# A layernorm head with its residual adds in line, and a softmax normaliser whose Ln and Exp stand two steps apart

## The chip, the cores and the metric

The kernel runs on all 8 cores of one Trainium2 chip. Each core computes one of the 8 batch elements and they exchange nothing. The time is the device time of the slowest core in microseconds (us).

## What is computed

Per batch element x is 2048 tokens by 1024 features. The layer is an attention block on the normalised x, then a three-matrix linear block with tanh on the normalised result, each added back:

```python
x = x + attn(layernorm(x))
#   attn(x): q, k, v = x@Wq, x@Wk, x@Wv in 16 heads of 64
#            softmax(q k^T / 8) v, heads joined, then x + out @ Wp
x = x + ffn(layernorm(x))
#   ffn(x): tanh(((x @ W1) @ W2) @ W3 + bias)
```

The attention block adds its own input back, so after it x holds x + layernorm(x) + out @ Wp.

## The kernel before

Everything lies transposed on the chip, features on the partitions. `xr` is the f32 residual in 8 blocks of 128 features by 2048 tokens; `S`, `qb`, `kb` and `vt` hold bf16 of the same size. The program is written by hand with one counting semaphore for each engine: TE (TensorE, PE in the profile), VE (VectorE, DVE), SE (ScalarE, ACT), GP (GpSimd, POOL) and SP. Each engine works its own queue in program order, so an instruction that waits holds back all that stand behind it on its engine.

**Head.** `layernorm` sums x and its square over the features with matmuls against ones, and gets mean and rstd for all 2048 tokens (rstd by Ln and Exp on ACT, L253 and L255). Then it goes over 8 blocks j: subtract the mean (L264, DVE), multiply by rstd (L280, or L272 for j of 5 and over, DVE), cast into `S` (L282 or L274, ACT), add the normalised block to the residual (L284, DVE), and 8 matmuls of the first quarter of Wq (L290, PE). For j = 5, 6, 7 the product goes to three spare f32 buffers in `kb`, and the add to the residual is left for after the loop (L310). The first copies of the projected q (L306, L307, ACT) wait for the last of these matmuls, and for `s_ve.n`, the last DVE instruction issued up to that point. The subtraction of j = 0 is queued ahead of DVE's wait for rstd. The other quarters of Wq, then Wk, Wv and a bound for the exponent follow. The first write to `kb` by the K projection waits for the adds that were left.

**Attention loop.** 512 iterations in the order (c, p, m): 4 chunks c of 512 query tokens, 8 head pairs p, 16 blocks m of 128 keys. Iteration t issues on ACT exp(t), the 128x1024 exponential (L866); on PE the scores of t+2 (L628, L632, called qk here), then the products with V (L878, L883, called pv) and the sums of the exponentials (L888, L891, called dn) of t. Scores and exponentials have two slots each, by the parity of m. So exp(t+2) needs qk(t+2) and dn(t), and qk(t+2) needs exp(t).

After m = 15 of a head pair DVE copies the two accumulators out (L899, L901). I call this a boundary; there are 32, the last of them behind the loop. pv of the next m = 0 waits for both copies. In the iteration m = 1 that follows, `_norm` is called: ACT gets Ln (L906) and Exp (L908) of the sums, which makes their reciprocal, and DVE multiplies (L914) and writes the bf16 result `ao`.

**Side work.** When the last pair of a chunk is normalised, the rest of the layer for that chunk is put in two lists that are worked off in the next chunk: 8 output projections (`wp_q`, L650) and 55 pieces in `work_q`, of which an even share is emitted by iteration number (`budget`). The first piece flushes all of `wp_q`, so the 8 projections come as one burst of 64 matmuls, at m = 2 of p = 0. By the formula for `budget`, of the later pieces these stand near a boundary, by p and m: statistics at m = 0 and 2 of p = 1 and 2; `emit_apply` (two blocks, each L754 and L757, DVE) at p = 3, m = 0, 3 and 5, all of which the first W1 projection at m = 7 needs (L776, PE); projections at m = 1 and 3 of p = 4 and 5 (L776) and at m = 1 of p = 6 (L794); a Tanh piece (L807, ACT) at p = 6, m = 4 and at p = 7, m = 2. For the last chunk the same work runs after the loop.

Lines as numbered in the kernel before:

Of the kernel before, what the change touches and what calls it, by code (L numbers as in the profile page):

```python
# [17 lines left out]
NCH = D // 128  # L18
# [33 lines left out]
def build_program(upto=99, dbg=False):  # L52
# [19 lines left out]
    with ctx:  # L72
# [143 lines left out]
        def layernorm(src_f32_j, dst_bf16, add_back, dma_gate=False, wq0=False):  # L216
# [7 lines left out]
            with nc.psum_tensor(_nm("ln_mean"), [128, 2048], F32) as mps, \  # L224
                 nc.psum_tensor(_nm("ln_sq"), [128, 2048], F32) as sps:
                mm_mark = [0, 0]
                for j in range(NCH):
# [9 lines left out]
                    for n4 in range(4):  # L237
# [17 lines left out]
                rstd_mark = s_se.inc(SE.activation(rstd_sb, rstd_sb, AF.Exp,  # L255
                                                   bias=0.0, scale=-0.5))
            def _normalize(wq0_pj):
                wsl0 = use_wquarter(0) if wq0_pj is not None else None
                mkq0 = 0
                deferred = []  # L260
                for j in range(NCH):
# [4 lines left out]
                    if j == 0:  # L266
                        VE.wait_ge(s_se.h, rstd_mark)
                    if add_back:
                        sl2 = j % 2
                        if j >= 5:  # L270
                            buf = kbf[:, 2048 * (j - 4):2048 * (j - 3)]
                            m = s_ve.inc(VE.tensor_mul(buf, tmpf, rstd_sb))  # L272
                            SE.wait_ge(s_ve.h, m)
                            cast_mark[sl2] = s_se.inc(SE.copy(dst_jj, buf))  # L274
                            VE.wait_ge(s_ve.h, m)
                            deferred.append((src_jj, buf))
                        else:
                            if cast_mark[sl2]:
                                VE.wait_ge(s_se.h, cast_mark[sl2])
                            m = s_ve.inc(VE.tensor_mul(tmpf2pp[sl2], tmpf, rstd_sb))  # L280
                            SE.wait_ge(s_ve.h, m)
                            cast_mark[sl2] = s_se.inc(SE.copy(dst_jj, tmpf2pp[sl2]))  # L282
                            VE.wait_ge(s_ve.h, m)
                            m = s_ve.inc(VE.tensor_add(src_jj, src_jj, tmpf2pp[sl2]))  # L284
                            VE.wait_ge(s_ve.h, m)
                        if wq0_pj is not None:
                            TE.wait_ge(s_se.h, cast_mark[sl2])
                            for half in range(2):
                                for n4 in range(4):
                                    ins = TE.matmul(  # L290
                                        wq0_pj[half][:, 512 * n4:512 * (n4 + 1)],
                                        wsl0[:, j, 128 * half:128 * (half + 1)],
                                        dst_bf16[:, 2048 * j + 512 * n4:
                                                 2048 * j + 512 * (n4 + 1)],
                                        start=(j == 0), stop=(j == NCH - 1),
                                        skip_group_check=True)
                            mkq0 = s_te.inc(ins)
                    else:
                        m = s_ve.inc(VE.tensor_mul(dst_jj, tmpf, rstd_sb))
                        VE.wait_ge(s_ve.h, m)  # L300
# [7 lines left out]
                add_done = 0  # L308
                for src_jj, buf in deferred:
                    add_done = s_ve.inc(VE.tensor_add(src_jj, src_jj, buf))  # L310
                    VE.wait_ge(s_ve.h, add_done)
                return (ev0, ev1, add_done)
# [44 lines left out]
        wproj(0, S_ap, qb_ap, q0=1, ev_init=ln_evs[:2])  # L357
# [4 lines left out]
        with nc.psum_tensor("pk0", [128, 1024], F32) as pk0, \  # L362
# [49 lines left out]
            for q in range(4):  # L412
                widx = 4 + q
                wsl = use_wquarter(widx)
                for jj in range(2):
                    j = 2 * q + jj
                    for hf in range(2):
# [14 lines left out]
                        if j == 0 and hf == 0 and ln_evs[2]:  # L432
                            SE.wait_ge(s_ve.h, ln_evs[2])
# [147 lines left out]
        with nc.psum_tensor("sc0", [128, 1024], F32) as sc0, \  # L581
# [274 lines left out]
            pending_norm = []  # L856
            TE.wait_ge(s_ve.h, s_ve.n)
# [3 lines left out]
            for t, (c, p, m) in enumerate(iters):  # L861
# [33 lines left out]
                if m == NM - 1:  # L895
# [8 lines left out]
                    def _norm(cp=c, pp=p, dncp=dn_cp):  # L904
                        SE.wait_ge(s_ve.h, dncp)
                        m1 = s_se.inc(SE.activation(dr, dr, AF.Ln, bias=0.0, scale=1.0))  # L906
                        SE.wait_ge(s_se.h, m1)
                        m1 = s_se.inc(SE.activation(dr, dr, AF.Exp, bias=0.0, scale=-1.0))  # L908
                        VE.wait_ge(s_se.h, m1)
                        while wp_q:  # L910
                            wp_q.pop(0)()
                        if cp > 0:
                            VE.wait_ge(s_te.h, st["wp_mm"])
                        mm = s_ve.inc(VE.tensor_mul(ao[:, 512 * pp:512 * (pp + 1)],  # L914
                                                    ao_un, dr))
                        if pp == NCH - 1:
                            ao_ready[cp] = mm
                            wp_q.extend(lambda j=j2: emit_wp_j(cp, j) for j2 in range(NCH))
                            work_q_done[0] = 0
                            work_q.extend(tail_thunks(cp, flush=(cp == NCC - 1)))  # L920
                            work_q_len[0] = len(work_q)
                        return mm

                    pending_norm.append(_norm)
                if pending_norm and m == 1:
                    ao_mult_mark = pending_norm.pop(0)()
# [7 lines left out]
            preload_flush_vt()  # L934
            while pending_norm:
                ao_mult_mark = pending_norm.pop(0)()
# [69 lines left out]
```

## Time and profile before

| | us |
|---|---|
| median of the runs shown (2) | 1306.75 (1306.47 to 1307.04) |
| profiled execution | 1306.87 |
| its span, slowest core (core 2) | 1305.2 |
| spans of the 8 cores | 1289.8 to 1305.2 |
| stages of core 2: head up to the first L344 | 0 to 117.8 |
| attention loop | 344 to 1201 |

The span runs from the first to the last instruction of a core; 1.7 us of the profiled execution lie outside it. TensorE is busy 76% of the span, ACT 55%, DVE 32%. In the attention loop chunk 0 (344 to 512 us) has no side work; chunks 1 to 3 take about 230 us each. The granted clock is a share of 2.4 GHz: 1.0 is 2.4 GHz and 0.5 is 1.2 GHz.

### The profile page before, as it was taken

How to read it: one execution, taken by the hardware profiler on the slowest of the kernel's cores; microseconds unless marked ns; L12 is line 12 of the kernel's file. 1: busy time of each engine (PE TensorE's matmuls, PEld its weight loads, DVE VectorE, ACT ScalarE, POOL GpSimd, SP SyncE). 2: the span in 40 equal slices, each digit the busy share in tenths (PEclk: the TensorE clock that was granted, in tenths of full speed). 3: DMA queues.
4: the chain of work that ended last, by engine and by line, in shares of the span. 5: the costliest groups of instructions: out<-in, count | busy, mean ns of one | idle time of the engine just before them, and what ended most of it. 6: DMA issues, size and time to landing. Idle time of an engine off the chain costs nothing.

```text
span 1305.2 us, 15441 instructions; the slowest of 8 cores (1289.8 to 1305.2 us)
## 1 busy us (share of the span) xinstructions
PE 988.1 (76%) x5111; PEld 334.2 (26%) x5185; DVE 415.6 (32%) x558; ACT 724.3 (55%) x702; POOL 66.9 (5%) x80
## 2 busy tenths in 40 slices
PE   3356977987678777787987777798778779976776
PEld 1112423443122222222222222232222223321222
DVE  3695033144510101234222223422222342222454
ACT  0223234101688987497677648766772986687102
POOL 2000000000000000000100010010001001211000
PEclk9768999999698999999999899999888999988878
DMA  9900000022000000401443350055334004593902
GB/s 251 168 1 0 1 1 1 1 33 33 1 1 1 1 1 2 64 1 17 65 58 59 63 65 2 6 63 70 58 65 65 1 2 64 67 161 52 143 1 64
DMA packets 98937, 57.65 MB, mean 44 GB/s; under 512 B 3624, under 2 KB 97840, under 8 KB 97840
## 3 DMA queue, kind: packets, MB, share of 16 engines
q0 software_dynamic: 79040, 39.85, 24.4%
q1 hardware_dynamic: 19824, 16.83, 4.4%
q8 instruction: 46, 0.75, 0.2%
q14 instruction: 27, 0.22, 0.1%
HBM read 88.12 MB, written 8.39 MB: 74 GB/s over the span
## 4 chain that ended last, share of the span: by engine, by line
PE 47%; ACT 17%; DVE 9%; issue 7%; DMA 2%; ACTq 0%; DVEq 0%; POOLq 0%
ACT S L866 14%; PE sc L628 9%; PE pvs L878 9%; PE dns L888 6%; PE lnps L776 4%; PE wps L776 4%; PE pvb L470 2%; PE pva L470 2%; PE wps L650 2%; PE lnps L794 2%; PE lnps L650 2%; DMA wbuf<-wp 2%; PE wps L794 1%; DVE tiny L544 1%; DVE S L899 1%
## 5 line engine op out<-in xcount | busy, mean ns | idle before, releaser
L866 ACT ACTIVATE S<-sc,cbias 128x1024 bf16<-128x1024 f32 x512 | 550.2, 1109 | 188.1 <-PE dns L891 175.4
L628 PE MATMUL sc<-qb,kb 64*128 64x512 bf16 x512 | 200.8, 393 | 121.4 <-ACT S L866 110.5
L878 PE MATMUL pvs<-S,vt 128*64 128x512 bf16 x512 | 212.8, 416 | 26.4 <-DVE S L901 26.4
L883 PE MATMUL pvs<-S,vt 128*64 128x512 bf16 x512 | 213.5, 417 | 0.0
L632 PE MATMUL sc<-qb,kb 64*128 64x512 bf16 x512 | 204.9, 401 | 0.0
L891 PE MATMUL dns<-S,ones 128*64 128x512 bf16 x512 | 202.5, 396 | 0.0
L888 PE MATMUL dns<-S,ones 128*64 128x512 bf16 x512 | 202.4, 395 | 0.0
L628 PEld LDWEIGHTS sc<-qb,kb 64*128 64x128 bf16 x512 | 47.6, 93 | 342.8 <-issue 342.8
L878 PEld LDWEIGHTS pvs<-S,vt 128*64 128x64 bf16 x512 | 54.9, 107 | 149.7 <-issue 149.6
L899 DVE COPY S<-pvs 128x512 f32<-128x512 f32 x32 | 22.1, 692 | 190.4 <-PE dns L891 186.4
L423 PE MATMUL pk<-S,vt 128*128 128x512 bf16 x250 | 57.7, 385 | 2.7 <-PEq L355 2.4
L524 ACT ACTIVATE S<-kb 128x2048 bf16<-128x2048 bf16 x8 | 15.1, 1906 | 76.6 <-PE tp L494 73.9
L139 POOL DMA_DIRECT2D wbuf<-w x36 | 31.5, 876 | 505.5 <-PE sc L632 437.8
L891 PEld LDWEIGHTS dns<-S,ones 128*64 128x64 bf16 x512 | 57.2, 112 | 0.0
L888 PEld LDWEIGHTS dns<-S,ones 128*64 128x64 bf16 x512 | 57.1, 112 | 0.1
L883 PEld LDWEIGHTS pvs<-S,vt 128*64 128x64 bf16 x512 | 55.0, 107 | 0.0
L632 PEld LDWEIGHTS sc<-qb,kb 64*128 64x128 bf16 x512 | 47.5, 93 | 0.0
L344 PE MATMUL pj<-S,vt 128*128 128x512 bf16 x188 | 43.0, 389 | 4.1 <-ACT qb L307 3.9
L434 ACT CAST kb<-pk 128x1024 bf16<-128x1024 f32 x16 | 16.2, 1012 | 51.4 <-PE pk L423 51.4
L807 ACT ACTIVATE S<-S,bias_pp_sb 128x512 bf16<-128x512 bf16 x32 | 23.1, 722 | 38.7 <-DVE S L802 38.6
L650 PE MATMUL wps<-S,wbuf 128*128 128x512 bf16 x97 | 30.7, 464 | 18.2 <-DMA wbuf<-wp 12.0
L290 PE MATMUL pq0a<-S,vt 128*128 128x512 bf16 x31 | 13.3, 568 | 40.3 <-ACT S L282 32.1
(162 smaller groups left out, 1147.1 us busy)
## 6 DMA issues: line engine op xcount, KB each, us to landing
wbuf<-w POOLq DMA_DIRECT2D x36, 512.0 KB, 5.6
xr<-x SPq DMA_DIRECT2D x4, 2048.0 KB, 24.4
out<-xr SPq DMA_DIRECT2D x128, 64.0 KB, 1.7
wbuf<-wp POOLq DMA_DIRECT2D x14, 512.0 KB, 6.0
vt<-w POOLq DMA_DIRECT2D x8, 512.0 KB, 20.4
vt<-wq POOLq DMA_DIRECT2D x4, 512.0 KB, 34.0
vt<-wk POOLq DMA_DIRECT2D x4, 512.0 KB, 47.5
wbuf<-wv POOLq DMA_DIRECT2D x4, 512.0 KB, 30.3
```

The source lines that it names most:

```text
L344: ins = TE.matmul(pj[sl][:, 512 * n4:512 * (n4 + 1)], wsl[:, i, 128 * jj:128 * (jj + 1)], src_bf[:, 2048 * i + 512 * n4: 2048 * i + 512 * ...
L423: ins = TE.matmul(pj[sl][:, 512 * n2:512 * (n2 + 1)], wsl[:, i, 128 * jj:128 * (jj + 1)], S_ap[:, 2048 * i + 1024 * hf + 512 * n2: 2048 * ...
L470: ins = TE.matmul(pvh[h][:, 512 * n2:512 * (n2 + 1)], wsl[:, i, 128 * jj:128 * (jj + 1)], S_ap[:, 2048 * i + 1024 * h + 512 * n2: 2048 * i ...
L628: TE.matmul(scs[sl][:, 0:512], kb[0:64, 2048 * p + 128 * m: 2048 * p + 128 * (m + 1)], qb[0:64, 2048 * p + 512 * c: 2048 * p + 512 * (c + 1)],
L632: ins = TE.matmul(scs[sl][:, 512:1024], kb[64:128, 2048 * p + 128 * m: 2048 * p + 128 * (m + 1)], qb[64:128, 2048 * p + 512 * c: 2048 * p ...
L650: ins = TE.matmul(acc[:], wsl[:, i, 128 * jj:128 * (jj + 1)], ao[:, 512 * i:512 * (i + 1)], start=(i == 0), stop=(i == NCH - 1))
L776: ins = TE.matmul(acc[:], wsl[:, i, 128 * jj:128 * (jj + 1)], rhs_of(i), start=(i == 0), stop=(i == NCH - 1))
L866: ins = SE.activation(p_un[sl], scs[sl][:], AF.Exp, bias=cbias[:], scale=0.125)
L878: TE.matmul(pvs[0:64, :], vt[:, 1024 * m + 128 * p: 1024 * m + 128 * p + 64], p_un[sl][:, 0:512], start=(m == 0), stop=(m == NM - 1), tile ...
L883: TE.matmul(pvs[64:128, :], vt[:, 1024 * m + 128 * p + 64: 1024 * m + 128 * (p + 1)], p_un[sl][:, 512:1024], start=(m == 0), stop=(m == NM ...
L888: TE.matmul(dns[0:64, :], ones64[:], p_un[sl][:, 0:512], start=(m == 0), stop=(m == NM - 1), tile_position=(0, 0), skip_group_check=True)
L891: ins = TE.matmul(dns[64:128, :], ones64[:], p_un[sl][:, 512:1024], start=(m == 0), stop=(m == NM - 1), tile_position=(0, 64), skip_group_ ...
```

## The change

In the head, DVE waits for rstd before the first subtraction and not after it. All 8 blocks take the path that j = 0 to 4 took: product in one of two alternating buffers, cast on ACT, add to the residual at once. The adds after the loop go, and so does the wait of the K projection for them. `SE.wait_ge(s_ve.h, s_ve.n)` ahead of L306 stays; the last DVE instruction issued there is now the add of j = 7, where it was the product of j = 7.

In the attention loop `_norm` is cut in two. Ln is still issued at m = 1. Exp, the wait of DVE for it, the product and, after the last pair of a chunk, the filling of `wp_q` and `work_q` are issued at m = 3, ahead of that iteration's side work. So the burst of output projections comes at m = 3 of p = 0. Behind the loop Ln and the rest run one after the other, as before. The number of instructions of each kind is the same.

```diff
@@ -252,37 +252,26 @@ layernorm
-                rstd_mark = s_se.inc(SE.activation(rstd_sb, rstd_sb, AF.Exp,
-                                                   bias=0.0, scale=-0.5))
+                m = s_se.inc(SE.activation(rstd_sb, rstd_sb, AF.Exp, bias=0.0, scale=-0.5))
+                VE.wait_ge(s_se.h, m)
             def _normalize(wq0_pj):
...
-                deferred = []
                 for j in range(NCH):
...
                     m = s_ve.inc(VE.tensor_sub(tmpf, src_jj, mean_sb))
                     VE.wait_ge(s_ve.h, m)
-                    if j == 0:
-                        VE.wait_ge(s_se.h, rstd_mark)
                     if add_back:
                         sl2 = j % 2
-                        if j >= 5:
-                            buf = kbf[:, 2048 * (j - 4):2048 * (j - 3)]
-                            m = s_ve.inc(VE.tensor_mul(buf, tmpf, rstd_sb))
-                            SE.wait_ge(s_ve.h, m)
-                            cast_mark[sl2] = s_se.inc(SE.copy(dst_jj, buf))
-                            VE.wait_ge(s_ve.h, m)
-                            deferred.append((src_jj, buf))
-                        else:
...
+                        if cast_mark[sl2]:
+                            VE.wait_ge(s_se.h, cast_mark[sl2])
+                        m = s_ve.inc(VE.tensor_mul(tmpf2pp[sl2], tmpf, rstd_sb))
+                        SE.wait_ge(s_ve.h, m)
+                        cast_mark[sl2] = s_se.inc(SE.copy(dst_jj, tmpf2pp[sl2]))
+                        VE.wait_ge(s_ve.h, m)
+                        m = s_ve.inc(VE.tensor_add(src_jj, src_jj, tmpf2pp[sl2]))
+                        VE.wait_ge(s_ve.h, m)
@@ -305,11 +294,7 @@
                 ev0 = s_se.inc(SE.copy(qb_ap[:, 0:2048], wq0_pj[0][:]))
                 ev1 = s_se.inc(SE.copy(qb_ap[:, 2048:4096], wq0_pj[1][:]))
-                add_done = 0
-                for src_jj, buf in deferred:
-                    add_done = s_ve.inc(VE.tensor_add(src_jj, src_jj, buf))
-                    VE.wait_ge(s_ve.h, add_done)
-                return (ev0, ev1, add_done)
+                return (ev0, ev1)
@@ -429,8 +414,6 @@ the K projection
-                        if j == 0 and hf == 0 and ln_evs[2]:
-                            SE.wait_ge(s_ve.h, ln_evs[2])
@@ -901,29 +885,37 @@ the attention loop
-                    def _norm(cp=c, pp=p, dncp=dn_cp):
+                    def _norm_ln(cp=c, pp=p, dncp=dn_cp):
                         SE.wait_ge(s_ve.h, dncp)
-                        m1 = s_se.inc(SE.activation(dr, dr, AF.Ln, bias=0.0, scale=1.0))
-                        SE.wait_ge(s_se.h, m1)
-                        m1 = s_se.inc(SE.activation(dr, dr, AF.Exp, bias=0.0, scale=-1.0))
-                        VE.wait_ge(s_se.h, m1)
-                        while wp_q:
-                            wp_q.pop(0)()
...
+                        lnm = s_se.inc(SE.activation(dr, dr, AF.Ln, bias=0.0, scale=1.0))
+
+                        def _norm_fin(cp=cp, pp=pp, lnm=lnm):
+                            SE.wait_ge(s_se.h, lnm)
+                            m1 = s_se.inc(SE.activation(dr, dr, AF.Exp,
+                                                        bias=0.0, scale=-1.0))
+                            VE.wait_ge(s_se.h, m1)
+                            while wp_q:
+                                wp_q.pop(0)()
+                            if cp > 0:
+                                VE.wait_ge(s_te.h, st["wp_mm"])
+                            mm = s_ve.inc(VE.tensor_mul(ao[:, 512 * pp:512 * (pp + 1)],
+                                                        ao_un, dr))
...
+                            return mm
+                        return _norm_fin
+                    pending_norm.append(_norm_ln)
+                if pending_fin and m == 3:
+                    ao_mult_mark = pending_fin.pop(0)()
                 if pending_norm and m == 1:
-                    ao_mult_mark = pending_norm.pop(0)()
+                    pending_fin.append(pending_norm.pop(0)())
@@ -932,8 +924,10 @@ after the loop
             preload_flush_vt()
+            while pending_fin:
+                ao_mult_mark = pending_fin.pop(0)()
             while pending_norm:
-                ao_mult_mark = pending_norm.pop(0)()
+                ao_mult_mark = pending_norm.pop(0)()()
```

## Rows read from the trace of the kernel before

**Rows 1.** the profile page's first line, of the whole program
```profile
span 1305.2 us, 15441 instructions; the slowest of 8 cores (1289.8 to 1305.2 us)
```

**Rows 2.** the page's chain that ended last, share by engine
```profile
PE 47%; ACT 17%; DVE 9%; issue 7%; DMA 2%; ACTq 0%; DVEq 0%; POOLq 0%
```

**Rows 3.** groups by line: busy us, mean ns, idle before and releaser
```profile
L866 ACT ACTIVATE S<-sc,cbias 128x1024 bf16<-128x1024 f32 x512 | 550.2, 1109 | 188.1 <-PE dns L891 175.4 <-PE sc L632 8.0 <-PE lnps L679 0.3
...
L906 ACT ACT_TABLE_LOAD x9 | 11.5, 1283 | 2.8 <-DVE S L901 2.7
```

**Rows 4.** timeline, VectorE, head: start us, duration, line, tiles, idle before
```profile
60.41 2.29 DVE L280 TENSOR_TENSOR qb<-qb 128x2048 f32<-128x2048 f32 x1 [3.29 <-ACT qb L255]
...
82.12 2.29 DVE L280 TENSOR_TENSOR kb<-qb 128x2048 f32<-128x2048 f32 x1 [0.17 <-DVE qb L264]
...
89.38 2.29 DVE L280 TENSOR_TENSOR qb<-qb 128x2048 f32<-128x2048 f32 x1 [0.17 <-DVE qb L264]
...
96.57 2.29 DVE L272 TENSOR_TENSOR kb<-qb 128x2048 f32<-128x2048 f32 x1
...
106.15 2.29 DVE L272 TENSOR_TENSOR kb<-qb 128x2048 f32<-128x2048 f32 x1
108.55 7.09 DVE L310 TENSOR_TENSOR xr<-xr,kb 128x2048 f32<-128x2048 f32 x3
```

**Rows 5.** the same timeline, ScalarE, end of the head
```profile
108.53 1.90 ACT L274 CAST S<-kb 128x2048 bf16<-128x2048 f32 x1 [2.89 <-DVE kb L272]
114.02 1.87 ACT L306 CAST qb<-pq0a 128x2048 bf16<-128x2048 f32 x1 [3.59 <-PE pq0b L290]
```

**Rows 6.** timeline, all engines, the boundary at 429.8 us
```profile
429.78 0.69 DVE L899 COPY S<-pvs 128x512 f32<-128x512 f32 x1 [16.96 <-PE dns L891]
...
431.36 0.63 ACT L906 ACTIVATE S<-S 128x512 f32<-128x512 f32 x1 [0.54 <-DVE S L901]
...
431.66 0.38 PE L891 MATMUL dns<-S,ones 128*64 128x512 bf16 x1
...
432.09 0.63 ACT L908 ACTIVATE S<-S 128x512 f32<-128x512 f32 x1
...
432.62 2.10 ACT L866 ACTIVATE S<-sc,cbias 128x1024 bf16<-128x1024 f32 x2
...
433.86 0.37 PE L628 MATMUL sc<-qb,kb 64*128 64x512 bf16 x1 [0.95 <-ACT S L866]
...
434.91 2.12 ACT L866 ACTIVATE S<-sc,cbias 128x1024 bf16<-128x1024 f32 x2 [0.19 <-PE dns L891]
```

**Rows 7.** timeline, VectorE: first copy of three other boundaries of chunk 0
```profile
409.10 0.69 DVE L899 COPY S<-pvs 128x512 f32<-128x512 f32 x1 [18.27 <-PE dns L891]
...
449.83 0.69 DVE L899 COPY S<-pvs 128x512 f32<-128x512 f32 x1 [16.32 <-PE dns L891]
...
469.87 0.69 DVE L899 COPY S<-pvs 128x512 f32<-128x512 f32 x1 [16.31 <-PE dns L891]
```

**Rows 8.** busy by stretch: length, PE, PEld, DVE, ACT, POOL, granted clock, DMA
```profile
411.20:414.60 3.40, 3.14 (x14) 0.60 (x12) 0.69 (x1) 2.84 (x4) 0.00 (x0) 0.50 0.00 0
```

**Rows 9.** timeline, all engines, after the boundary at 595.7 us
```profile
600.11 0.69 DVE L914 TENSOR_TENSOR S<-S 128x512 bf16<-128x512 f32 x1
...
600.71 0.68 DVE L754 TENSOR_TENSOR vtmp<-xr,vtmp 128x512 f32<-128x512 f32 x1
...
607.33 1.67 PE L776 MATMUL wps<-S,wbuf 128*128 128x512 bf16 x7 [0.97 <-DVE S L757]
```

**Rows 10.** timeline, TensorE, after the boundary at 622.2 us
```profile
625.30 1.90 PE L776 MATMUL wps<-S,wbuf 128*128 128x512 bf16 x8
...
627.13 0.39 PE L628 MATMUL sc<-qb,kb 64*128 64x512 bf16 x1
```

**Rows 11.** timeline, ScalarE, after the boundary at 708.4 us
```profile
713.67 1.28 ACT L807 ACT_TABLE_LOAD   x1
...
715.59 2.10 ACT L866 ACTIVATE S<-sc,cbias 128x1024 bf16<-128x1024 f32 x2
```

More of the change, by code:

```diff
@@ L265, in _normalize @@
                     VE.wait_ge(s_ve.h, m)
-                    if j == 0:
-                        VE.wait_ge(s_se.h, rstd_mark)
                     if add_back:
                         sl2 = j % 2
-                        if j >= 5:
-                            buf = kbf[:, 2048 * (j - 4):2048 * (j - 3)]
-                            m = s_ve.inc(VE.tensor_mul(buf, tmpf, rstd_sb))
-                            SE.wait_ge(s_ve.h, m)
-                            cast_mark[sl2] = s_se.inc(SE.copy(dst_jj, buf))
-                            VE.wait_ge(s_ve.h, m)
-                            deferred.append((src_jj, buf))
-                        else:
[L278 to L285, printed above, removed]
+                        if cast_mark[sl2]:
[6 more added lines that the diff above has]
+                        VE.wait_ge(s_ve.h, m)
                         if wq0_pj is not None:
@@ L355, in wproj @@
             nc.all_engine_barrier()
-        wproj(0, S_ap, qb_ap, q0=1, ev_init=ln_evs[:2])
+        wproj(0, S_ap, qb_ap, q0=1, ev_init=ln_evs)
         rmax = tiny[:, 0:2]
@@ L856, in build_program @@
             pending_norm = []
+            pending_fin = []
             TE.wait_ge(s_ve.h, s_ve.n)
@@ L902, in build_program @@
                     recip_mark = dn_cp
-                    def _norm(cp=c, pp=p, dncp=dn_cp):
+                    def _norm_ln(cp=c, pp=p, dncp=dn_cp):
                         SE.wait_ge(s_ve.h, dncp)
-                        m1 = s_se.inc(SE.activation(dr, dr, AF.Ln, bias=0.0, scale=1.0))
-                        SE.wait_ge(s_se.h, m1)
-                        m1 = s_se.inc(SE.activation(dr, dr, AF.Exp, bias=0.0, scale=-1.0))
-                        VE.wait_ge(s_se.h, m1)
-                        while wp_q:
-                            wp_q.pop(0)()
[L912 to L922, printed above, removed]
@@ L924, in build_program @@
-                    pending_norm.append(_norm)
+                        lnm = s_se.inc(SE.activation(dr, dr, AF.Ln, bias=0.0, scale=1.0))
[10 more added lines that the diff above has]
+                                                        ao_un, dr))
+                            if pp == NCH - 1:
+                                ao_ready[cp] = mm
+                                wp_q.extend(lambda j=j2: emit_wp_j(cp, j)
+                                            for j2 in range(NCH))
+                                work_q_done[0] = 0
+                                work_q.extend(tail_thunks(cp, flush=(cp == NCC - 1)))
+                                work_q_len[0] = len(work_q)
+                            return mm
```

## The prediction, made before the changed kernel was run

> **What bounds the kernel now.** I read the page's first line, then the chain that ended last, then the groups by line, then the two places that the change touches in the timeline. The slowest core spans 1305.2 us [rows 1]. The chain lies for 47% on PE, 17% on ACT and 9% on DVE [rows 2]: no engine bounds the whole, the work is handed from one to another. So each edit has to be read where it stands.
>
> In the head DVE sets the pace. From block to block it takes 89.38 - 82.12 = 7.26 us, the subtraction, the product and the add of 2.29 us each with their issue. In the blocks that leave the add for later it takes (106.15 - 96.57)/2 = 4.79 us [rows 4]. ACT sits idle 2.89 us before the last cast [rows 5], so the cast waits for DVE.
>
> In chunk 0 of the loop it is a circle of ACT and PE. ACT has exponentials of 1.11 us, idle 188.1 us in front of them in total, 175.4 of it on L891, the dn matmuls [rows 3]. At the boundary at 429.78 [rows 6] the copies run, Ln starts at 431.36, Exp at 432.09, exp(2) at 432.62, qk(4) at 433.86 and exp(4) at 434.91. A boundary period is 469.87 - 449.83 = 20.04 us [rows 7].
>
> **The head, part by part.** *Subtraction behind the wait.* The product of j = 0 starts at 60.41, as soon as Exp is done, its subtraction having run before [rows 4]. Now the subtraction starts there and the product one DVE step later: 7.26 - 4.79 = 2.47 for a step with its wait, 2.4 without; I take 2.4. *Adds in line.* Between the product of j = 5 and that of j = 7 there are now two adds more, 2 x (7.26 - 4.79) = 4.94. The add of j = 4 was in line already and that of j = 7 comes behind the last cast. Together the last cast moves by 2.4 + 4.9 = 7.3, with the waits of the alternating buffers 7.4 us. *The copy L306.* It starts at 114.02, 5.5 us after the last cast [rows 5], and it would also wait for the add of j = 7. That add starts when the cast does and takes 2.3, so it is done first. *The adds taken away at the end.* Those 7.09 us at 108.55 [rows 4] run beside the matmuls and copies of Wq; nothing on the path waited, so nothing comes back. If the path from the cast to Wq had slack, the 7.4 would be less, but PE has only the head's own matmuls to do there and waits for the casts. Head: +7.4 us, between +7.3 and +7.5.
>
> **The loop, a boundary that is bound by latency.** The total of ACT's work stays; what changes is whether it fills a gap. Before, exp(2) waits for Ln and Exp. Without Exp it needs dn(0), which ends at 431.66 + 0.38 = 432.04, and starts 0.1 later, at 432.14 where it was 432.62: 0.48 earlier [rows 6]. Two exponentials in 2.10 us of 1.1 each start 1.00 apart, so exp(3) starts at 433.14 and Exp at 434.14. Exp holds ACT for 432.62 - 432.09 = 0.53, so exp(4) may start at 434.67. By PE it could start at 432.14 + (434.91 - 432.62) = 434.43. ACT decides: 434.67 for 434.91, a gain of 0.24 us, which the circle then carries on. The floor of this gain is 0, if Exp at m = 3 costs what m = 1 saves; the ceiling is Exp's whole 0.53.
>
> **All 31 boundaries inside the loop.** I went through each by the same rows and sorted them.
> - 11 are of this kind (chunk 0 from the fourth on, and those with statistics beside them): 11 x 0.24 = 2.6.
> - 3 in chunk 0 have the clock at 0.50 just behind them [rows 8]: PE decides there and has the earlier start; I take 0.3 each, 0.9.
> - 3 more, two at chunk ends and one with a table load, again set by the chain from exp(2): 0.3 each, 0.9.
> - 3 have a Tanh piece at m = 2. There ACT runs exp(2), a table load, Tanh and exp(3) back to back [rows 11], so exp(3), and behind it PE, come the whole 0.53 sooner: 1.6.
> - 8 have a projection at m = 1 or a long load: qk(4) at 627.13 stands right behind L776, which began at 625.30 [rows 10]. PE is the bound and ACT's 0.53 is worth 0.
> - 3, at p = 3, lose. DVE is the bound there: the product L914 at 600.11 goes between the apply pieces of m = 0 and m = 3, the next of which begins at 600.71, and the projection at 607.33 has PE idle 0.97 for the last L757 [rows 9]. Now L914 waits for Exp at m = 3. By the steps of the clean boundary exp(2) starts 432.14 - 429.78 = 2.36 behind the first copy [rows 6], here at 598.07, exp(3) at 599.07 and Exp at 600.07; Exp takes 0.63 and DVE follows 0.1 behind, at 600.80 in place of 600.11: 0.69 later, and the whole apply chain with it. -0.69 each, -2.1. Bounds: 0 if Exp came no later, -1.2 if exp(3) were late by half a step.
>
> The burst of projections at a chunk's start is issued one iteration later. Its first matmul needs L914, which would end about 0.3 us after PE is free; but PE has then done one iteration more ahead of the burst, so this is within the gain taken. The loads of wp stay where they were.
>
> What is late next: DVE's product comes some 2 us later at every boundary. Behind it on DVE stand only side pieces from m = 3 on; those of m = 1 and 2 now go ahead of it. Its readers are the burst, once a chunk, and the next copies 12 iterations later.
>
> **Sum.** Loop: 2.6 + 0.9 + 0.9 + 1.6 + 0 - 2.1 = 3.9 us gained. Net 7.4 - 3.9 = +3.5. Against the profiled execution of 1306.87, which is 0.12 over the median of the runs, that is **1310.4 us**.
>
> **A rule on tables.** The switch between Ln and Tanh shows 9 loads at L906, 1.283 us each [rows 3]. The load at 713.67 is followed by Tanh and exp(3) 1.92 later, 1.28 and 0.64, with no further hold [rows 11]; and among the 512 exponentials of L866 [rows 3] the view has no load, though they run after Ln and after Tanh alike. So Exp on either side of a Tanh finds its table, and the number of loads stays. The Trainium skill ("ScalarE: Activation LUTs", section "What ACT_TABLE_LOAD costs") gives 2.66 us for every switch, 1.28 of load and 1.38 of drain. The load agrees with the trace, the drain does not show. Were it there, and a switch in each of the 3 places where a Tanh now comes between Ln and Exp, two switches in each would by that page be an estimated 16 us, and the time 1326.
>
> **Rivals.**
> 1. *The loop gives back the full Exp everywhere.* 31 x 0.53 = 16.4, no loss at p = 3: 1306.9 + 7.4 - 16.4 = 1297.9. For it: ACT idles at many boundaries. Against: Exp still takes ACT 0.53 at m = 3, and 8 boundaries are PE's. About 0.07.
> 2. *The split gains nothing, DVE's losses stay.* 1306.9 + 7.4 + 2.1 = 1316.4. For it: the total of ACT's work is the same. Against: exp(2) is plainly held by 0.48. About 0.15.
> 3. *The head's delay is hidden.* 1306.9 - 3.9 = 1303.0. Only if something else held Wq; ACT's idle time before the last cast speaks against it. About 0.05.
> 4. *The tables.* If Exp behind a Tanh wants the table of Ln back, that is two loads in each of 3 places, 6 x 1.28 = 7.7: 1318.1. About 0.03.
> 5. *The clock.* This is the one that ends on the slower side. Place: the iterations just after a boundary. One stretch at 0.50 [rows 8] makes the period 429.78 - 409.10 = 20.68 [rows 6, 7] in place of 20.04, 0.64 more. If ACT's second hold at m = 3 made PE pause twice and brought a new such stretch to all 28 boundaries that I did not count with one, 28 x 0.64 = 18 us: 1328, and 1337 with half as much again where PE is the bound. From 0.81 us lost at each boundary ((26.1 - 3.5)/28) it passes 2%. Against: PE's pauses get shorter, not longer. About 0.06, 0.02 of it past 2%.
>
> The forecast has 0.64. A difference of 2%, about what a measurement of this kernel can tell from no change, is 26 us. Rival 1 is 0.7% faster and rival 2 is 0.7% slower, so nearly all is within it: faster 0.01, same 0.97, slower 0.02. The range for 8 in 10: the forecast with its bounds is 1306 to 1314; reaching to rivals 2 and 3 it is 1303 to 1317.
>
> **What would show it.** L280 for j = 0 at 62.8 and the last cast at 115.9, L306 at 121.4, all seven product starts in between 7.26 apart. At a clean boundary exp(2) about 2.36 after the first copy, where it was 2.84, and exp(4) 4.9 after it, where it was 5.13; a clean period of 19.8. At p = 3, L776 waits 1.7 and more for L757 in place of 0.97. L906 still has 9 loads and L908 none. I would be wrong if L306 moved by less than 7, if the clean period stayed at 20.04 or fell to 19.5, or if the share of half clock in the loop changed, as that is set by PE's pauses and one such stretch is worth as much as two or three boundaries.

## The result

The changed kernel takes 1312.43 us in the median of 17 runs, the kernel before 1307.08 us in 16. The ratio is 1.0037, with a 95% interval of 1.0025 to 1.0049: 4.8 us slower. The medians are of all executions; in some of them the cores of one die were granted a lower clock and the time was up to 9% longer, and the ratios and the means below leave these out. The forecast was 1310.4 us, ratio 1.003, within a range of 1303 to 1317. The sign and the size were right; of the terms behind the sum, the head and five kinds of boundary came out about as worked, and three kinds did not, one of them (p = 0) by no more than its periods scatter.

The page of the changed kernel, its first line and the chain that ended last by engine:

```profile
span 1313.2 us, 15517 instructions; the slowest of 8 cores (1298.7 to 1313.2 us)
...
PE 49%; ACT 15%; DVE 9%; issue 6%; DMA 2%; DVEq 0%; ACTq 0%; POOLq 0%
```

The profiled execution took 1314.77 us and its slowest core is core 7, where before it was core 2 with 1305.2 [rows 1]. The spans of the eight cores of one execution lie some 15 us apart, and which core is the slowest changes from one execution to the next, so I compare the same core or the mean of all eight below. That mean is 1297.4 us in the profiled execution of before and 1305.8 in that of the changed kernel. PE's share of the chain rose from 47% to 49% and ACT's fell from 17% to 15% [rows 2].

Two groups of the groups by line, core 2 of the changed kernel (busy us, mean ns, idle before and releaser):

```profile
L850 ACT ACTIVATE S<-sc,cbias 128x1024 bf16<-128x1024 f32 x512 | 548.8, 1110 | 192.5 <-PE dns L875 178.4 <-PE sc L615 8.4
...
L890 ACT ACT_TABLE_LOAD x9 | 11.5, 1283 | 2.8 <-DVE S L885 2.7
```

ACT's exponentials are as before and the table loads at Ln are still 9 of 1.283 us [rows 3]; there is no load at L894, the Exp that was moved. Where a Tanh now comes between Ln and Exp, ScalarE of the same core shows:

```profile
715.30 1.28 ACT L790 ACT_TABLE_LOAD   x1
716.60 0.72 ACT L790 ACTIVATE S<-S,bias_pp_sb 128x512 bf16<-128x512 bf16 x1
717.23 1.10 ACT L850 ACTIVATE S<-sc,cbias 128x1024 bf16<-128x1024 f32 x1
718.22 0.62 ACT L894 ACTIVATE S<-S 128x512 f32<-128x512 f32 x1
```

The Tanh starts 1.30 us behind the start of its load, and the moved Exp at 718.22 needs none.

**Head.** The timeline of core 2 in the head, VectorE and then ScalarE:

```profile
61.27 2.29 DVE L263 TENSOR_TENSOR qb<-xr,qb 128x2048 f32<-128x2048 f32 x1 [5.48 <-ACT qb L255]
63.67 2.29 DVE L269 TENSOR_TENSOR qb<-qb 128x2048 f32<-128x2048 f32 x1
```

```profile
59.26 1.91 ACT L255 ACTIVATE qb<-qb 128x2048 f32<-128x2048 f32 x1
...
116.79 1.90 ACT L271 CAST S<-kb 128x2048 bf16<-128x2048 f32 x1 [5.36 <-DVE kb L269]
122.50 1.86 ACT L295 CAST qb<-pq0a 128x2048 bf16<-128x2048 f32 x1 [3.81 <-PE pq0b L279]
```

The first subtraction starts at 61.27, when rstd is there; before, the product started at that point [rows 4]. From rstd to the last cast it is 116.79 - 61.27 = 55.52 us, before 108.53 - 60.41 = 48.12 [rows 4, 5]: +7.40. The mean of the eight cores is +7.40 too. The copy of q follows 5.7 us behind the cast, before 5.5 [rows 5].

**A clean boundary**, core 2, the same place in a chunk as [rows 6]:

```profile
452.69 0.69 DVE L883 COPY S<-pvs 128x512 f32<-128x512 f32 x1 [14.01 <-PE dns L875]
...
454.27 0.63 ACT L890 ACTIVATE S<-S 128x512 f32<-128x512 f32 x1 [0.54 <-DVE S L885]
...
455.04 2.12 ACT L850 ACTIVATE S<-sc,cbias 128x1024 bf16<-128x1024 f32 x2
...
456.30 0.37 PE L611 MATMUL sc<-qb,kb 64*128 64x512 bf16 x1 [0.48 <-ACT S L850]
...
457.05 0.63 ACT L894 ACTIVATE S<-S 128x512 f32<-128x512 f32 x1
...
457.57 1.11 ACT L850 ACTIVATE S<-sc,cbias 128x1024 bf16<-128x1024 f32 x1
...
457.78 0.69 DVE L901 TENSOR_TENSOR S<-S 128x512 bf16<-128x512 f32 x1 [3.60 <-ACT S L894]
```

exp(2) starts 455.04 - 452.69 = 2.35 us behind the first copy, before 432.62 - 429.78 = 2.84 [rows 6]. Exp, L894, now stands between exp(3) and exp(4), and exp(4) starts 4.88 behind the copy, before 5.13. The period, from two copies two boundaries apart:

```profile
432.90 0.69 DVE L883 COPY S<-pvs 128x512 f32<-128x512 f32 x1 [14.01 <-PE dns L875]
...
472.48 0.69 DVE L883 COPY S<-pvs 128x512 f32<-128x512 f32 x1 [14.01 <-PE dns L875]
```

(472.48 - 432.90)/2 = 19.79, before 20.04 [rows 7]. That is 0.25 us won, and 0.24 was worked out.

**p = 3**, core 2:

```profile
597.51 0.69 DVE L883 COPY S<-pvs 128x512 f32<-128x512 f32 x1 [2.22 <-PE dns L875]
...
602.67 0.69 DVE L901 TENSOR_TENSOR S<-S 128x512 bf16<-128x512 f32 x1 [0.69 <-PE sc L615]
...
603.28 0.69 DVE L737 TENSOR_TENSOR vtmp<-xr,vtmp 128x512 f32<-128x512 f32 x1
...
609.90 1.46 PE L759 MATMUL wps<-S,wbuf 128*128 128x512 bf16 x6 [1.99 <-DVE S L740]
```

The product L901 starts 602.67 - 597.51 = 5.16 behind the first copy, before 600.11 - 595.7 = 4.4 [rows 9]; the next apply piece stands right behind it, and PE is idle for 1.99 us before the projection, where it was 0.97.

**All boundaries.** The table gives the change of a period (from one boundary's first copy to the next), mean over the eight cores and, for p = 0 to 7, over chunks 1 to 3, worked out from the starts of that copy in the profiled executions. That is one execution of each kernel, and some periods differ between executions of the same code: in six kernels below that leave Exp at m = 1 at the chunk start, or move it only to m = 2, the period of p = 0 comes out 0.2 to 1.0 us longer than in this one of before.

| period that begins at | forecast, us | changed kernel, us |
|---|---|---|
| chunk 0, seven together | -1.9 | -3.3 |
| p = 0 (chunk start) | -0.3 | +0.35 |
| p = 1 | -0.24 | -0.19 |
| p = 2 | -0.24 | +0.76 |
| p = 3 | +0.69 | +0.90 |
| p = 4, p = 5 | 0, 0 | 0.00, -0.09 |
| p = 6 | -0.1 | 0.00 |
| p = 7 (Tanh between Ln and Exp) | -0.53 | -0.36 |

The loop's sum in these executions is -3.3 + 3 x 1.37 = +0.8 us where -3.9 was forecast. The first exponential of the loop starts 7.8 us later, mean of the cores; 0.4 of that is a later rstd. Together that is the +8.5 of the mean span in the two profiled executions. Over all the executions behind the ratio the kernel is 4.8 us slower, so with the head at 7.4 the loop is nearer -2.6 there: the profiled pair shows the loop worse than the timed executions do.

### The profile page after: what moved, and what is told of

Same layout as the page of the kernel before. It is cut to its first block, busy times and chain, and to the rows that moved or that the text cites. A ratio compares the mean times of both kernels' runs of the same rounds, so it can differ in the third digit from the quotient of the medians.

```text
span 1313.2 us, 15517 instructions; the slowest of 8 cores (1298.7 to 1313.2 us)
## 1 busy us (share of the span) xinstructions
PE 999.8 (76%) x5185; PEld 334.9 (26%) x5185; DVE 415.1 (32%) x558; ACT 719.5 (55%) x702; POOL 66.8 (5%) x80
## 4 chain that ended last, share of the span: by engine, by line
PE 49%; ACT 15%; DVE 9%; issue 6%; DMA 2%; DVEq 0%; ACTq 0%; POOLq 0%
ACT S L850 12%; PE sc L611 10%; PE pvs L862 9%; PE dns L872 6%; PE lnps L759 4%; PE wps L759 4%; PE lnps L777 2%; PE pva L453 2%; PE pvb L453 2%; PE wps L633 2%; PE wps L777 2%; PE lnps L633 2%; DMA wbuf<-wp 2%; DVE tiny L527 1%; DVE S L883 1%
## 5 line engine op out<-in xcount | busy, mean ns | idle before, releaser
L611 PE MATMUL sc<-qb,kb 64*128 64x512 bf16 x512 | 199.9, 391 | 111.9 <-ACT S L850 100.9
L611 PEld LDWEIGHTS sc<-qb,kb 64*128 64x128 bf16 x512 | 47.4, 93 | 335.9 <-issue 335.9
```

The source lines that it names most:

```text
L611: TE.matmul(scs[sl][:, 0:512], kb[0:64, 2048 * p + 128 * m: 2048 * p + 128 * (m + 1)], qb[0:64, 2048 * p + 512 * c: 2048 * p + 512 * (c + 1)],
```

## The experiments

Theory A, my forecast mended by the trace after: the head costs its 7.4 us in full, each clean boundary wins 0.25, and the loss in chunks 1 to 3 comes from Exp standing too late at p = 2 and p = 3, part of it by more half clock (stretches with a granted clock of 0.50). Rivals are named in the expectations. All ratios are to the kernel before on the same chip; "cores" is the difference of the mean over all eight spans of the timed executions, known to 1 to 2 us. exp_m4, sub_late and adds_inline were run for their profile and have no ratio.

| kernel | ratio, 95% interval | cores, us |
|---|---|---|
| split_only | 0.9988 (0.9975 to 1.0001) | -1.8 |
| head_only | 1.0054 (1.0040 to 1.0068) | +7.3 |
| exp_m2 | 0.9995 (0.9984 to 1.0006) | +0.4 |
| keep_p23 | 0.9972 (0.9953 to 0.9991) | -3.6 |
| chunk0_only | 0.9963 (0.9951 to 0.9976) | -3.6 |
| split_select | 0.9936 (0.9921 to 0.9951) | -8.1 |
| select_again | 0.9962 (0.9949 to 0.9976) | -5.8 |
| start_only | 0.9999 (0.9985 to 1.0014) | -1.1 |
| late_only | 0.9999 (0.9989 to 1.0010) | -0.4 |

### The two halves of the change

**split_only** is the kernel before with the loop's part of the diff alone.

> The kernel before with only the loop's change (Ln at m = 1, Exp at m = 3), the head as before. Theory A (the head costs its 7.4 us in full, the loop is near zero: 0.24 us won at each clean boundary, lost again at p = 2 and p = 3 where Exp now comes late, and in more half clock): about 2 to 4 us under the changed kernel's ratio minus the head, that is 1304 to 1308 where before is 1307, ratio 0.998 to 1.001. Theory B (the loop gives the 3.9 us of the forecast and the head costs over 8): 1303 or less, ratio 0.997 or less. In the trace by A: clean period of chunk 0 19.8 us, the period that ends at the p = 3 boundary's successor 0.78 longer than before, and the period before it 0.25 to 1.1 longer.

**head_only** is the kernel before with the head's part alone.

> The kernel before with only the head's change, the loop as before. Theory A: every core's first copy of the projected q starts 7.4 us later than before and the whole is 7 to 8 us slower, 1314 to 1315 where before is 1307, ratio 1.0055 to 1.006. Theory B (the head costs over 8 because the clock falls in it): ratio 1.0065 and more. Were the head's delay partly hidden: under 1.004.

Measured: -1.8 us by the cores for the loop and +7.3 for the head. Together +5.5, and the ratio of the changed kernel says +4.8: the parts add, within 1 to 2 us. In split_only's profiled execution the loop is 1.1 us longer than in that of before, in the timed ones the whole is 1.8 shorter: that the loop lies between -3 and +1 us is what can be said of it. The head costs what was worked out, and theory B is out: the loop does not give 3.9 us, and for the head, whose ratio's interval just reaches theory B's 1.0065, the trace has 7.40.

### The head's two edits

```diff
 sub_late
                 rstd_mark = s_se.inc(SE.activation(rstd_sb, rstd_sb, AF.Exp, ...))
+                VE.wait_ge(s_se.h, rstd_mark)
```

> The kernel before with one edit: DVE waits for rstd ahead of the first subtraction. Both theories: the product of j = 0 and everything behind it in the head move by one DVE step, 2.4 us; the copy L306 (114.0 before in the profiled core) at 116.4 give or take the 1 us by which cores differ; the whole +2.4, 1309.5.

**adds_inline** is head_only with the wait for rstd put back behind the first subtraction.

> The kernel before with the other half of the head's change: the adds of j = 5 to 7 in line, the first subtraction still ahead of the wait for rstd. The copy L306 moves by 4.9 to 5.0 us beside the product of j = 0, the whole by the same: 1311 to 1312.

VectorE and ScalarE of core 2 in sub_late:

```profile
59.39 2.29 DVE L265 TENSOR_TENSOR qb<-xr,qb 128x2048 f32<-128x2048 f32 x1 [5.48 <-ACT qb L255]
61.86 2.29 DVE L281 TENSOR_TENSOR qb<-qb 128x2048 f32<-128x2048 f32 x1 [0.18 <-DVE qb L265]
```

```profile
109.98 1.90 ACT L275 CAST S<-kb 128x2048 bf16<-128x2048 f32 x1 [2.89 <-DVE kb L273]
```

and in adds_inline:

```profile
61.59 2.29 DVE L270 TENSOR_TENSOR qb<-qb 128x2048 f32<-128x2048 f32 x1 [3.29 <-ACT qb L255]
```

```profile
114.71 1.90 ACT L272 CAST S<-kb 128x2048 bf16<-128x2048 f32 x1 [5.36 <-DVE kb L270]
```

From rstd to the last cast sub_late takes 109.98 - 59.39 = 50.59 us and adds_inline 114.71 - 61.59 = 53.12, before 48.12: +2.47 and +5.00. Their sum is 7.47, the whole change has 7.40. The places expected for L306 (116.4 and about 119) were missed, 114.94 and 120.41: rstd comes 1 to 2 us earlier or later from one execution to the next, and from the last cast to L306 it is 4.0 to 5.7 us, depending on the core. The distance from rstd to the last cast is what is steady. The total times were missed too, 1312.0 us for 1309.5 in sub_late and 1324.3 for 1311 to 1312 in adds_inline; each is a single execution, and the eight cores of adds_inline lie between 1303 and 1323 us, so they decide nothing.

### Where Exp may stand

```diff
 exp_m2 (and exp_m4 with 4), on split_only
-                if pending_fin and m == 3:
+                if pending_fin and m == 2:
```

> Head as before, Ln at m = 1, Exp and the product at m = 2 in place of m = 3. If the losses at p = 2 and p = 3 come from Exp standing behind exp(3), they go: at p = 3 DVE has its product by 600.1 as before (0 instead of +0.78 a chunk), at p = 2 exp(4) comes no later than before. The clean boundary keeps 0.24, since exp(2), Exp, exp(3) fill the same 2.5 us. The boundaries with a Tanh at m = 2 lose what the split won there. Theory A: 2 to 5 us under split_only, ratio to before 0.995 to 0.998. Rival (the losses in chunks 1 to 3 are the clock's own, by chance of the core): the same as split_only within 1 us.

> Head as before, Exp and the product at m = 4 in place of 3. The boundary closes on the exponential of m = 15, so only the chain of odd m counts. Theory P (parity): at m = 2 and m = 4 Exp stands right ahead of an odd exponential and holds it, at m = 3 it stands ahead of an even one. So the clean period of chunk 0 is 20.0 to 20.1 us here, as with Exp at m = 2, although exp(2), exp(3) and exp(4) start earlier than before. Theory D (distance): what counts is that Exp is past the slow iterations 0 to 2, and then the period is 19.8 or less.

ScalarE of exp_m2, core 2, at a clean boundary whose first copy starts at 444.40, and VectorE's first copies of that boundary and the one before:

```profile
446.76 1.11 ACT L867 ACTIVATE S<-sc,cbias 128x1024 bf16<-128x1024 f32 x1
447.77 0.62 ACT L911 ACTIVATE S<-S 128x512 f32<-128x512 f32 x1
448.29 2.11 ACT L867 ACTIVATE S<-sc,cbias 128x1024 bf16<-128x1024 f32 x2
```

```profile
424.31 0.69 DVE L900 COPY S<-pvs 128x512 f32<-128x512 f32 x1 [15.31 <-PE dns L892]
...
444.40 0.69 DVE L900 COPY S<-pvs 128x512 f32<-128x512 f32 x1 [15.31 <-PE dns L892]
```

The same of exp_m4, boundary at 468.34:

```profile
470.69 2.12 ACT L867 ACTIVATE S<-sc,cbias 128x1024 bf16<-128x1024 f32 x2
473.00 1.11 ACT L867 ACTIVATE S<-sc,cbias 128x1024 bf16<-128x1024 f32 x1 [0.19 <-PE dns L892]
474.01 0.62 ACT L911 ACTIVATE S<-S 128x512 f32<-128x512 f32 x1
474.53 2.11 ACT L867 ACTIVATE S<-sc,cbias 128x1024 bf16<-128x1024 f32 x2
```

```profile
448.24 0.69 DVE L900 COPY S<-pvs 128x512 f32<-128x512 f32 x1 [13.01 <-PE dns L892]
...
468.34 0.69 DVE L900 COPY S<-pvs 128x512 f32<-128x512 f32 x1 [13.01 <-PE dns L892]
```

In exp_m2 exp(2) starts 2.36 behind the copy and exp(4) 4.9, both as early as at m = 3, but Exp holds exp(3) until 3.89, where it was 3.83. The period is 444.40 - 424.31 = 20.09. In exp_m4 exp(2), exp(3) and exp(4) are all earlier than before, exp(4) at 473.00 - 468.34 = 4.66, and Exp holds exp(5) until 6.19, before 6.14. The period is 468.34 - 448.24 = 20.10. Distance is out and parity holds: the next boundary waits for the exponential of m = 15, so only the chain of odd m counts, each 2.3 us behind the last but one. At a clean boundary Exp is free where it pushes an even exponential.

That was a miss of the expectation for exp_m2, which kept 0.24 at the clean boundary. It also missed p = 2, where periods without any half clock are 22.35 us with Exp at m = 2, 21.61 at m = 3 and 21.46 before, and the total, 0.9995 where 0.995 to 0.998 was expected. Its part on p = 3 held: the period changed by -0.02 there, in place of +1.34 in split_only.

What costs at p = 3 is DVE's queue. With Exp at m = 3 the product waits for it, idle for 0.69 us, and the apply pieces of m = 3 stand behind the product. exp_m4 shows that lateness alone does no harm. VectorE of its core 2, boundary at 596.91:

```profile
603.87 0.69 DVE L757 TENSOR_TENSOR S<-vtmp 128x512 bf16<-128x512 f32 x1
604.48 0.68 DVE L918 TENSOR_TENSOR S<-S 128x512 bf16<-128x512 f32 x1
605.08 0.68 DVE L754 TENSOR_TENSOR vtmp<-xr,vtmp 128x512 f32<-128x512 f32 x1
```

The product L918 comes 7.57 us behind the copy, later than in any other kernel, but the pieces of m = 3 were put in the queue ahead of it, DVE does not idle, and the period is 26.51 us as before. With Exp at m = 3 it is 27.29 in 22 of the changed kernel's 24 cases, +0.78. The rest of +0.90, and most of the rest of split_only's +1.34, is half clock: in 2 and 8 of 24 cases a stretch of 3.4 us at half clock begins 12.7 us behind the copy, 0.5 us behind the start of the projection that PE had waited to begin, and the period is 28.88. No kernel with the period at 26.51 has a stretch at that place.

### Which boundaries win and which lose

All of these are split_only with one more line: at the boundaries named, Exp and the product are called at m = 1, together with Ln.

```diff
-                    pending_fin.append(pending_norm.pop(0)())
+                    fin1 = pending_norm.pop(0)()
+                    if c > 0 and p in (2, 3):         # keep_p23
+                        ao_mult_mark = fin1()
+                    else:
+                        pending_fin.append(fin1)
```

In the diff c and p are of the pair that has just begun. In chunk0_only the condition is `c > 0 or p == 0`, in split_select and select_again `c > 0 and p in (1, 2, 3, 4, 5)`, in start_only `not (c > 0 and p == 0)`, in late_only `not (c > 0 and p in (6, 7))`.

> Head as before, Ln at m = 1 and Exp at m = 3, but at the boundaries at which p is 2 or 3 in chunks 1 to 3 Exp and product stay at m = 1 as in the kernel before: 6 boundaries of 31. Theory A: those two periods of each chunk fall back to the lengths of before (-0.8 and -1.0 on average), so 4 to 6 us under split_only, ratio to before 0.995 to 0.998. Rival: no difference to split_only beyond 1 us, the losses then lie in the burst or in the clock elsewhere.

> Head as before; Ln and Exp stand apart (m = 1 and m = 3) only at the 7 boundaries inside chunk 0, everywhere else they stay together at m = 1. Theory A: each of the 7 periods is 0.25 us shorter, 20.04 to 19.79, and the rest is the kernel before: -1.8 us, ratio 0.998 to 0.999; and the chunks with side work keep the half clock of before (about 20 us a chunk, where split_only has 25). Rival, the half clock in chunks 1 to 3 comes from where the loop stands against the chip's clock once chunk 0 has become shorter: then it rises here too.

> Head as before; split (m = 1 and m = 3) in chunk 0, at the chunk starts (p = 0) and at p = 6 and 7 of the later chunks, and together at m = 1 at p = 1 to 5, where the split cost time or did nothing. Theory A: -1.8 in chunk 0, about -0.5 at each p = 7 period and nothing lost elsewhere, so at least as fast as keep_p23: ratio 0.996 to 0.998, best guess -4 us. Rival: no better than chunk0_only.

> The same kernel as split_select, beside its two parts on one chip. If its -8 us is the sum of parts, chunk0_only -4, start_only and late_only make up the rest; if the parts sum to -6 or less, the rest is scatter or the way in which the boundaries stand to the half-clock stretches. Ratio 0.993 to 0.996.

> Head as before; the split only at the three chunk starts (p = 0 of chunks 1 to 3), which also puts the burst of output projections at m = 3. Forecast's step: 0.3 us won at each, -0.9 in all, ratio 0.999 to 1.0. Theory S: split_select was 4.5 us under chunk0_only by the mean over cores, more than p = 6 and 7 can give, so the starts give about 1 us each: -3, ratio 0.997 to 0.998, with the p = 0 period 1 us shorter on average.

> Head as before; the split only at the six boundaries with p = 6 and p = 7 of chunks 1 to 3. Forecast's step: 0.3 where ACT is the bound at p = 6 and 0.53 at each p = 7, so -0.4 to -0.5 in each p = 7 period, as after and split_only show: -1.5 us, ratio 0.998 to 0.9995. Theory S: the same. Rival: -3 and more, if Ln alone ahead of the Tanh also saves in p = 6.

What was measured, again as the change of a period in us, mean of cores and chunks, one profiled execution each. The last two columns count, at the p = 2 boundaries (24 of them) and in chunk 0 (56), those with a stretch at half clock that begins 1.4 to 4 us (in chunk 0 to 4.6) behind the first copy.

| kernel | chunk 0, seven | p = 0 | p = 2 | p = 3 | p = 7 | half at p = 2 | half in chunk 0 |
|---|---|---|---|---|---|---|---|
| before | 0 | 0 | 0 | 0 | 0 | 3 | 10 |
| changed | -3.3 | +0.35 | +0.76 | +0.90 | -0.36 | 18 | 0 |
| split_only | -3.4 | -0.19 | +0.85 | +1.34 | -0.44 | 16 | 0 |
| keep_p23 | -3.4 | -0.10 | +0.63 | +0.03 | -0.48 | 16 | 0 |
| exp_m2 | -0.5 | +0.62 | +0.29 | -0.02 | -0.26 | 3 | 16 |
| exp_m4 | +0.9 | +0.72 | +0.85 | -0.01 | -1.22 | 20 | 22 |
| chunk0_only | -3.4 | +0.86 | +0.14 | -0.02 | -0.04 | 3 | 0 |
| split_select | -3.4 | +0.20 | +0.72 | +0.03 | -0.49 | 16 | 0 |
| select_again | -3.4 | -0.46 | +0.77 | -0.01 | -0.36 | 15 | 0 |
| start_only | +0.8 | -0.04 | +0.58 | +0.02 | 0.00 | 13 | 15 |
| late_only | +0.1 | +0.44 | -0.09 | -0.02 | -0.42 | 1 | 10 |
| head_only | -0.8 | +0.17 | -0.02 | -0.02 | +0.11 | 1 | 7 |
| sub_late | +0.4 | +0.55 | -0.09 | +0.03 | -0.04 | 0 | 13 |
| adds_inline | -1.0 | +0.95 | +0.20 | +0.06 | +0.10 | 5 | 6 |

The last three leave the loop as it was, so they show how far a number here moves by itself. There are four readings.

*Chunk 0* gives 3.4 us, not 1.8: seven times 0.25, and 1.6 more because the half-clock stretches behind its boundaries are gone: 6 to 16 of 56 where Exp is at m = 1 or m = 2, 22 at m = 4, and 0 in each of the six executions with the split there at m = 3. So chunk0_only has 0.9963 where 0.998 to 0.999 was expected. PE pauses twice behind a clean copy, for the copies and ahead of qk(4). The pause for the copies in the kernel before, in the changed one and in exp_m2, PE of core 2:

```profile
431.42 0.38 PE L878 MATMUL pvs<-S,vt 128*64 128x512 bf16 x1 [1.06 <-DVE S L901]
```

```profile
454.32 0.38 PE L862 MATMUL pvs<-S,vt 128*64 128x512 bf16 x1 [1.06 <-DVE S L885]
```

```profile
425.94 0.38 PE L879 MATMUL pvs<-S,vt 128*64 128x512 bf16 x1 [1.36 <-DVE S L902]
```

The one ahead of qk(4), the row of L611 above, is 0.48 in all the split kernels and was 0.95 [rows 6]. The two add up to 2.01 us before, 1.84 in exp_m2 and exp_m4, and 1.54 with Exp at m = 3, the only one of the three without stretches. That fits, but no run varied the pauses alone, and the most stretches (22) do not go with the longest pauses, so the cause stays open.

*p = 3* is settled by keep_p23 too: with Exp back at m = 1 there, +0.03.

*p = 2* is not what I took it for. keep_p23 has Exp at m = 1 there and still loses 0.63, which leaves it 1.8 us under split_only by the cores and not 4 to 6, and start_only, which splits nowhere but at the chunk start, loses 0.58. The half-clock stretch behind the p = 2 boundary is there in 13 to 20 cases of 24 in every kernel that puts Exp and the burst of the chunk start at m = 3 or 4, and in 0 to 5 in every kernel that doesn't. So most of this loss is made two boundaries earlier, at the chunk start, and what is lost at p = 2 is the clock. At the chunk start Exp and the burst of projections move together in every one of these kernels, so which of the two does it is not shown. Core 3 of the changed kernel shows such a stretch. The first view is ScalarE behind the p = 2 boundary at 572.21, the second the busy time of two stretches (length, PE, PEld, DVE, ACT, POOL, granted clock, DMA share, GB/s):

```profile
574.56 1.11 ACT L850 ACTIVATE S<-sc,cbias 128x1024 bf16<-128x1024 f32 x1
576.50 1.11 ACT L850 ACTIVATE S<-sc,cbias 128x1024 bf16<-128x1024 f32 x1 [0.82 <-PE dns L875]
577.51 0.62 ACT L894 ACTIVATE S<-S 128x512 f32<-128x512 f32 x1
578.04 1.11 ACT L850 ACTIVATE S<-sc,cbias 128x1024 bf16<-128x1024 f32 x1
```

```profile
571.80:574.90 3.10, 1.44 (x11) 0.39 (x7) 2.14 (x4) 2.33 (x4) 0.00 (x0) 1.00 0.00 0
575.30:578.70 3.40, 3.40 (x15) 0.69 (x13) 1.14 (x3) 2.58 (x4) 0.00 (x0) 0.51 0.00 0
```

and ScalarE of core 3 before, its boundary at 567.43:

```profile
570.27 2.12 ACT L866 ACTIVATE S<-sc,cbias 128x1024 bf16<-128x1024 f32 x2
572.56 3.42 ACT L866 ACTIVATE S<-sc,cbias 128x1024 bf16<-128x1024 f32 x3 [0.16 <-PE dns L891]
```

exp(4) comes 578.04 - 572.21 = 5.83 us behind the copy, before 572.56 - 567.43 = 5.13. Ahead of exp(3) ACT waited 0.82 us for dn(1), in the stretch whose granted clock is 0.51. At cores 0, 4 and 7, which had no such stretch here, exp(3) starts at 3.85 as before and exp(4) at 5.38, Exp being behind an exp(3) that came no sooner. exp(4) is 0.25 later, and the period, where it has no half clock at all, 21.61 for 21.46: 0.15 lost, where I had written 0.24 won.

*The sum of parts.* chunk0_only -3.6, start_only -1.1 and late_only -0.4 make -5.1; select_again, beside the last two on one chip, has -5.8 and split_select on the chip of chunk0_only had -8.1. So the parts add within the scatter, and the same kernel differs by 2.3 us between the two chips. The first figure was below what was expected for split_select (0.996 to 0.998) and the second just above the 0.993 to 0.996 then expected. start_only's ratio of 0.9999 doesn't bear out theory S. The table says why: the six executions with the start split at m = 3 have the p = 0 period at -0.46 to +0.35, the rest with Exp at m = 1 there at 0 to +0.95, so some 0.5 us is won at p = 0, and 0.6 is lost at p = 2. late_only won 0.42 in each p = 7 period and its ratio doesn't show it: 1.3 us is below what 11 executions resolve. exp_m4's -1.22 at p = 7 goes with 3.4 us of half clock in 19 of 24 cases, where the kernel before has 6.8 us in all 24; it was not followed up.

split_select beats both kernels: 1300.44 us beside 1308.88, and again 1301.39 beside 1306.65. It is the head of before with the split only in chunk 0, at chunk starts and at p = 6 and 7. Against chunk0_only it was 4.5 us ahead on their common chip by the mean of the cores, and chunk0_only was not run on the other. A kernel with its other splits but none at the chunk start, which might also spare the half clock at p = 2, was not run.

## Why the prediction was right, and where

**The head** was right in every step: 2.4 for the subtraction (2.47), 4.9 for two adds (5.00), 7.4 in all (7.40), nothing given back for the adds taken away. Rival 3, that something hides it, is out: head_only is 1.0054, with its interval from 1.0040.

**The clean boundary** was right at 0.24 (0.25), and so was its reason, but not the whole of it: I followed exp(4), and it is exp(5) and the odd chain that close the period. At m = 3 both give 0.25. At m = 2 or 4 my argument would have given the same gain, and the runs show none.

**The three at p = 3** were right in mechanism: product late by 0.69 (0.77), period 0.78 longer in a core without a new half-clock stretch, and no loss when the product stands behind the apply pieces, at m = 4. **The eight where PE is the bound** were worth 0, as forecast. **The three with a Tanh** gave 0.36 to 0.49 us at each for 0.53. The loads stayed at 9 and none came at the moved Exp, so rival 4 is out. The 2.66 us that the Trainium skill gives for a switch ("ScalarE: Activation LUTs", section "What ACT_TABLE_LOAD costs") were not seen: the loads took 1.283 us each, and the activation behind starts 1.30 us after the load does, with no room for a drain.

**The step that failed** is the first item of the list, "11 of this kind", and in it the three at p = 2. I sorted them by where exp(4) stood, and it stood at 5.13 as in chunk 0. But exp(3) stood exactly at the release of dn(1), which lies behind a statistics matmul of m = 0. There exp(3) can't move, and Exp lands behind it, on the path: -0.24 should have been +0.15. On top came the half clock, which makes it +0.76 together; start_only, with Exp at m = 1 at p = 2, has +0.58 of that from the clock alone. The term of chunk 0 erred the other way, -1.9 for -3.3, all of it clock. I had counted 3 boundaries of chunk 0 with half clock from core 2; over the eight cores it is 10 of 56, and the sum gave nothing for their going. Rival 5 named the clock as the risk and placed it behind the second hold of ACT; it came behind the p = 2 boundaries instead, for a move made at p = 0, and in chunk 0, where Exp did move to m = 3, it went away.

In the profiled executions errors of 1.4 us one way and 6 us the other left +0.8 for the loop in place of -3.9; of the 6, 2 stand at p = 0 and are no more than the scatter of that period. Over the timed executions the loop is at about -2. So the total is right because the head carries it and its working held; that the loop's errors came to only 1 to 2 us in it is partly luck.

## What to carry to other kernels

Here splitting a serial pair on a shared engine paid only where the second half landed in a gap of the chain that closes the period: ask which slot's chain the end waits for, and whether the instruction ahead of the gap can itself move. Residual adds that nobody waits for belong behind the last instruction that somebody does wait for: here that was 5 us, and starting one operation ahead of a wait another 2.5. A deferred instruction also holds up what stands behind it in its own queue. Where that queue is the bound, as DVE's at p = 3, put it behind the pieces that are due (m = 4, no loss) or leave it early (m = 1 or 2, no loss), not between (m = 3, +0.78).

## What the runs showed of the hardware

The granted clock at a boundary can depend on what was moved long before it: with Exp and the burst of the chunk start at m = 3 and all else as before, the p = 2 boundaries with a half-clock stretch went from 3 to 13 of 24, some 65 us later in the kernel. The stretches are 3.4 us long, some twice that. What one costs depends on where it falls: nothing to 0.4 us early in a period of p = 3, about 1 us at p = 2, 1.2 in chunk 0, 1.6 behind the wait at p = 3.

The mean over the eight spans of an execution scatters less than the slowest core, but not by much: by a standard deviation of 1.3 us against 1.9 in 24 executions of the kernel before on one chip, 1.0 against 1.3 on a second, and 1.7 against 1.5 on a third.
